# Value blocks of a two-layer macaron kernel: all at full width, in every second slot, ahead of the second score

## What is computed

```python
q = moe_proj(Wq, bq).reshape(B, T, H, D)      # H = 16, D = 8
k = moe_proj(Wk, bk).reshape(B, T, H, D)
v = moe_proj(Wv, bv).reshape(B, T, H, D)
scores = jnp.einsum('bthd,bshd->bhts', q, k) / np.sqrt(D).astype(np.float32)
attn = jax.nn.softmax(scores, axis=-1)
out = jnp.einsum('bhts,bshd->bthd', attn, v).reshape(B, T, C)
return out @ Wo + bo

x = x + 0.5 * _L0_ffn_ref(_layernorm(x), ...)
x = x + _L0_attn_ref(_layernorm(x), ...)
x = x + 0.5 * _L0_ffn_ref(_layernorm(x), ...)
```

## Time and profile before

| what | value |
|---|---|
| median of three runs | 1281.38 us (1278.4 to 1283.0) |
| the profiled execution | 1280.69 us |
| its span, first to last instruction | 1279.0 us, mean granted TensorE clock 0.955 |
| busy over the span | PE 1157.0 us, VectorE 1061.4, ScalarE 941.1, GpSimd 307.7 |
| maximum reductions (L959) | 512, 594.5 us |
| exponentials (L795) | 1024, 545.3 us |
| value matmuls (L1261) | 3584, 317.1 us |
| score matmuls (L1245) | 1024, 309.2 us |
| maximum matmuls (L1230) | 1024, 282.6 us |

### The profile page before, as it was taken

One profiled execution on the slowest core, in us unless ns is written; L12 is line 12 of the kernel. 1 busy time (PEld: TensorE's weight loads), 2 busy tenths in 40 slices (PEclk: granted clock), 3 DMA queues, 4 the chain that ended last, 5 costly groups with the idle time before them and its releaser, 6 DMA issues. The chain is left out here.

```text
span 1279.0 us, 31986 instructions
## 1 busy us (share of the span) xinstructions
PE 1157.0 (90%) x10884; PEld 502.0 (39%) x10884; DVE 1061.4 (83%) x1787; ACT 941.1 (74%) x2001; POOL 307.7 (24%) x535
## 2 busy tenths in 40 slices
PE   4499999998987899999999999998769999999996
PEld 3122222222225555555566565555522222222223
DVE  6899999998987777777755777776589999998997
ACT  3179999998983677777755777775339999998994
POOL 4400000022000354444432444443330000000200
PEclk9689999999997999999999999998869999999998
DMA  4812212354210001000000000000431212244422
GB/s 109 247 32 56 64 52 60 81 88 85 66 41 19 18 23 29 18 17 18 18 18 18 18 18 18 18 18 2 149 99 48 69 47 55 75 79 88 83 48 67
DMA packets 51793, 69.55 MB, mean 54 GB/s; under 512 B 21168, under 2 KB 29296, under 8 KB 51696
## 3 DMA queue, kind: packets, MB, share of 16 engines
q1 hardware_dynamic: 51696, 68.26, 21.7%
HBM read 37.30 MB, written 22.54 MB: 47 GB/s over the span
## 5 line engine op out<-in xcount | busy, mean ns | idle before, releaser
L959 DVE TENSOR_REDUCE neg_max<-ps 128x1 f32<-128x1024 f32 x512 | 594.5, 1213 | 26.6 <-PE ps L1230 22.8
L795 ACT ACTIVATE arena<-ps 128x512 f32<-128x512 f32 x1024 | 545.3, 597 | 84.2 <-PE ps L1245 71.9
L1261 PE MATMUL ps<-arena 128*32 128x256 f32 (+1 forms) x3584 | 317.1, 426 | 25.0 <-ACT arena L795 24.2
L1245 PE MATMUL ps<-arena 50*128 50x512 bf16 x1024 | 309.2, 388 | 6.2 <-DMA arena<-max_dram 5.6
L1230 PE MATMUL ps<-arena 48*128 48x512 bf16 x1024 | 282.6, 397 | 16.8 <-DVE neg_max L959 14.4
L1031 DVE TENSOR_REDUCE a_neg_max<-ps 128x1 f32<-128x129 f32 (+7 forms) x256 | 191.9, 750 | 110.4 <-PE ps L1382 109.4
L634 POOL TENSOR_SCALAR arena<-arena,a_rsum 128x128 f32<-128x128 f32 (+7 forms) x256 | 191.1, 747 | 310.8 <-DVE a_rsum L1050 303.5
L731 ACT ACTIVATE arena<-ps,a_neg_max 128x129 f32<-128x129 f32 (+7 forms) x256 | 189.2, 739 | 51.0 <-DVE a_neg_max L1031 38.5
L1377 PE MATMUL ps<-arena 64*128 64x128 f32 (+6 forms) x512 | 192.6, 457 | 0.0
L1375 PE MATMUL ps<-arena 64*128 64x321 f32 (+7 forms) x512 | 187.9, 450 | 4.9 <-DVE neg_s_null L1062 1.9
L1245 PEld LDWEIGHTS ps<-arena 50*128 50x128 bf16 x1024 | 71.7, 94 | 258.2 <-ACT arena L795 226.3
(11 more groups left out here) (125 smaller groups left out, 820.5 us busy)
## 6 DMA issues: line engine op xcount, KB each, us to landing
arena<-stack_dram SPq DMA_DIRECT2D x128, 192.0 KB, 3.4
stack_dram<-arena SPq DMA_DIRECT2D x48, 256.0 KB, 3.8
o_dram<-arena SPq DMA_DIRECT2D x32, 256.0 KB, 2.1
arena<-arena SPq DMA_DIRECT2D x32, 256.0 KB, 3.6
arena<-o_dram SPq DMA_DIRECT2D x30, 256.0 KB, 4.4
arena<-max_dram SPq DMA_DIRECT2D x256, 1.0 KB
x<-in_L_attn_x SPq DMA_DIRECT2D x2, 512.0 KB, 4.9
max_dram<-max_T SPq DMA_DIRECT2D x64, 8.0 KB, 1.7
```

The source lines that it names most:

```text
L795: nc.scalar.activation(probs[:, t, :], ps[:, EXP_BANK[t], :], ACT.Exp, scale=F_SCALE).then_inc(probs_ready, 1)
L959: nc.vector.tensor_reduce(neg_max[:, g, t:t + 1], ps[:, bank:bank + 2, :].rearrange("p a b -> p (a b)"), AX, ALU.max, negate=True).then_in ...
L1245: ins = nc.tensor.matmul(ps[:, bank, :], stack[rows, g, 1, kt * P:(kt + 1) * P], stack[rows, g, 0, h * HALF:(h + 1) * HALF], start=True, s ...
L1261: ins = nc.tensor.matmul(ps[row:row + 32, PV_BANK, cols], v_unit[:, g, t // 2, :], probs[:, t, cols], start=j == 0 and c0 == 0 and g % 2 == 0,
```

## The change

The value groups 0, 1 and 2 are no longer cut in two. All four groups are full-width blocks of 512 queries: group 3 of the unit before in slot 1, as it was, and groups 0, 1 and 2 in slots 3, 5 and 7, each between that slot's maximum tile and its second score. The even slots have no value block. A group could start in the slot before, once its four exponentials are there; the new table puts it one slot behind that. The evacuation of the output bank moves behind the fourth exponential of a unit, where it stood behind the third. The block behind the last unit is the same one, read from the new table.

```diff
+        VALUES_AT = {kt: ((NT // 2 - 1 if kt == 1 else (kt - 3) // 2, 0, HALF),) if kt % 2 else () for kt in range(NT)}
...
-                    if t == 2 and g == 0 and not first:
+                    if t == 3 and g == 0 and not first:
                         evacuate(1, it - 1)
-                    if t == 2 and g == 2:
+                    if t == 3 and g == 2:
                         evacuate(0, it)
...
                     score_tile(g, it, kt, 0)
                     if ahead:
                         max_tile((g + AHEAD) % NB, it + (g + AHEAD) // NB, kt)
-                    if kt == 1 and not first:
-                        values((g - 1) % NB, it if g else it - 1, NT // 2 - 1, 0, HALF)
+                    for j, c0, c1 in VALUES_AT[kt]:
+                        if kt >= 3:
+                            values(g, it, j, c0, c1)
+                        elif not first:
+                            values((g - 1) % NB, it if g else it - 1, j, c0, c1)
                     score_tile(g, it, kt, 1)
-                    if kt >= 2:
-                        values(g, it, kt // 2 - 1, kt % 2 * (HALF // 2), (kt % 2 + 1) * (HALF // 2))
...
-                values(NB - 1, last, NT // 2 - 1, 0, HALF)
+                for kt in range(2):
+                    for j, c0, c1 in VALUES_AT[kt]:
+                        values(NB - 1, last, j, c0, c1)
```

## The result

The changed kernel takes 1334.78 us (median of four runs, 1329.48 to 1337.94) against 1281.6 for the kernel before (four executions too, one more than in the table above): a ratio of 1.041, 95% interval 1.039 to 1.044. It is slower by 53 us. The prediction said 1329, within 1312 to 1346. The profiled execution is the shortest of the four, 1329.48 us, 48.8 over the 1280.69 of before.

What follows compares the result with a forecast made beforehand. VectorE bounds the kernel before; the change makes a closed 2.60 us chain the bound. 21.5 + 21.9 + 1.3 + 2 x 1.15 + 2 x 0.6 = 48.2 us on 1280.69 gives 1329 us, range 1312 to 1346.

Steps and rivals of the forecast that it cites:

- The chain: Second score, exponential, released bank, next odd slot's value block, second score: 2.60 us for two slots, 10.40 a unit; chance 0.80.
- VectorE's 2.31: VectorE's floor for two slots: a unit's eight maxima and transpose cannot go below 9.23 us, a quarter being 2.31.
- Rival A: Faster: TensorE does 0.7 us a unit less and units fall from 9.55 to 9.23, giving 1265 us; chance 0.09.
- Across units: Over a unit's end the ring closes too, through bank 1, with the same link lengths, so 2.60 us there.
- The late units: Units held by row maxima arriving late from memory: between 0 and +2.5 us in all, +1.3 taken.
- The first units: Each layer's first unit, run at half clock: between nothing and 1.5 us more, +0.6 taken for each layer.
- The last two units of a layer: Units without maxima at a layer's end: said to run at most as much longer, with no term in the sum.
- The 1.15 for a layer's end: VectorE's closing work waits for the last output, whose evacuation leaves at 2.60 instead of 1.45: +1.15 us each layer.
- The evacuation: Output bank's evacuation behind the fourth exponential: TensorE free at 4.15, block due at 4.20, so hidden; otherwise under 2 us.
- B: No change: the ring of scores and blocks holds but comes out near 2.39 for two slots, 1281 us; chance 0.05.
- C: TensorE's brief waits make its clock fall and rise; ten units of sixty at half clock make 1391 us; chance 0.06.
- D: The change doesn't do what it says: none found; sign would be slot 3's block waiting over 0.1 us for the evacuation.

Runs made afterwards that it cites:

- the fastest version: Changed kernel with half-width value blocks, each one slot late between maximum tile and second score, plus output read-backs spread one to a unit: 1257.88 us, ratio 0.981.
- the second run: Changed kernel with its four full blocks moved behind the second score of the odd slots: 1333.97 us, ratio 1.039 to the kernel before.
- the first experiment: Changed kernel with half-width blocks between maximum tile and second score, one slot late, evacuation behind the fifth exponential: 1273.35 us, ratio 0.993 to the kernel before.
- ninth run: Kernel before with only the output read-back transfers spread one to a unit, value blocks untouched: 1275.32 us, ratio 0.995.

## Why the prediction was right, point by point

**The chain.** All four links came out as read from slot 1 of the kernel before: 0.43, 0.65, 0.53 and 1.00, 2.61 and not 2.60. That it closes, and is longer than VectorE's 2.31, is shown from four sides: by width (512, 384, 256), by one link less (the maximum tile), by one link more (the blocks a slot earlier), and by the place, which alone is worth 9 us at most. No run gives the ring a fourth bank, which would be the most direct test. Rival A's gain for TensorE shows in the value matmuls, 42 us less, but no one waited for it. Beside that, the rule that a change of tiling mode drains TensorE, in the Trainium skill's "TensorEngine Tiling (Array Packing)", Key Properties, cannot be the decisive one here: the fastest version has eight blocks a unit and so twice the changes of the slow one.

**Across units** the prediction said that the links are the same. In the loop they are not: 2.69, as the second of two scores that are released together leaves 0.08 behind the first. That is 0.08 for each unit in the loop. Together with the 0.01 in each chain, units came out at 10.5 and not 10.40. From the fourth exponential of unit 1 to that of unit 29, and at the ends of both layers and the start of the second, ScalarE's rows are:

```profile
83.37 2.06 ACT L796 ACTIVATE arena<-ps 128x512 f32<-128x512 f32 x4 [0.45 <-PE ps L1246]
...
377.41 2.07 ACT L796 ACTIVATE arena<-ps 128x512 f32<-128x512 f32 x4 [0.45 <-PE ps L1246]
...
404.58 0.60 ACT L796 ACTIVATE arena<-ps 128x512 f32<-128x512 f32 x1 [0.33 <-PE ps L1246]
...
975.00 2.62 ACT L796 ACTIVATE arena<-ps 128x512 f32<-128x512 f32 x5 [9.87 <-PE ps L1246]
...
1309.75 0.60 ACT L796 ACTIVATE arena<-ps 128x512 f32<-128x512 f32 x1 [0.33 <-PE ps L1246]
```

294.04 us in 28 units are 10.50 each. The same ends in the kernel before:

```profile
372.09 5.35 ACT L795 ACTIVATE arena<-ps 128x512 f32<-128x512 f32 x10 [0.16 <-PE ps L1245]
...
951.55 2.62 ACT L795 ACTIVATE arena<-ps 128x512 f32<-128x512 f32 x5 [9.98 <-PE ps L1245]
...
1255.61 5.35 ACT L795 ACTIVATE arena<-ps 128x512 f32<-128x512 f32 x10 [0.16 <-PE ps L1245]
```

**The sum.** The 29 units of a layer gained 24.3 and 24.8 us, where the prediction had 21.5 and 21.9: this term was sized too small, by the 0.1 above. The late units were given 1.3, between 0 and 2.5, and took nothing: the longer unit hides them whole (the one wait for row maxima left in the trace is ahead of the second layer's first unit, and all units in the loop take 10.4 to 10.5). The first units took 1.8 more and 0.4 less, in place of 0.6 each; this goes with when the clock comes up (8.4 and 8.0 us behind the layer's first exponential before, 11.9 and 5.2 now). The last two units of a layer took 1.5 more.

The 1.15 for a layer's end has a size near this, but not its reason. The evacuation that VectorE's closing work needs did leave later, 0.95 behind its old place in the unit (at 2.40 behind the first exponential; before, 1.45), yet the closing work came 0.7 us earlier in the unit: 10.7 behind unit 30's first exponential (1290.89 to 1301.60) and not 11.4; in the first layer likewise. In both kernels the store of that output stands in SyncE's queue behind four transfers of row maxima, and starts when they have been issued, not when the evacuation is over (at 1245.10 before, at 1293.88 now). These transfers come 0.6 us earlier in the unit than before:

```profile
1245.66 2.56 SPq L378 DMA_DIRECT2D arena<-max_dram  x4
1248.27 0.44 SPq L385 DMA_DIRECT2D o_dram<-arena  x1
...
1292.90 2.56 SPq L379 DMA_DIRECT2D arena<-max_dram  x4
1295.51 0.44 SPq L386 DMA_DIRECT2D o_dram<-arena  x1
...
1301.60 0.69 DVE L980 TENSOR_TENSOR arena<-arena 112x512 f32<-112x512 f32 x1 [3.70 <-DMA arena<-o_dram]
```

So that this term came out near is luck: what made the layer's end longer is the chain in the last two units, which the prediction named beside it and gave no term. The chain that ended last goes through VectorE's closing work in the kernel before, and through these units' last blocks in the changed one.

In all the two layers' scores take 27.7 us longer in the first (310.4 from 67.08 to 377.44, now 338.0 from 67.14 to 405.18) and 25.9 in the second: 53.6, against 48.2 predicted, and the difference of the medians is 53.

**What the sum did not hold.** The profiled execution is only 48.8 longer, since between the layers, where the code is the same, it took 569.8 (405.18 to 975.00) and the one of before 574.1 (377.44 to 951.55), and the part behind the second layer's last exponential 0.6 less. Over the eleven profiles of this study that stretch takes 569 to 574 us, with the stretches at half clock in other places each time. So an execution of this kernel carries some us that no edit made, and the nearness of 48.2 and 48.8 is partly luck: one term too small, one of the right size for another reason, one stretch short.

**The evacuation** is hidden as said, "by a hair": the block of slot 3 in a unit with evacuation follows its first score by the usual 0.53 (220.53 to 221.06), and the old place would have cost 0.2 to 0.28 in every second unit.

**The rivals.** A and B asked for a chain of 2.31 or 2.39; it was 2.61. Two experiments whose chain was brought to 2.4 came within 8 and 13 us of B's time, their late units included, so its threshold was about right. C did not come about in the changed kernel's mid-layer (clock 1.00 in the window above), but it did at the end of a layer in two other runs with full blocks. The clock of the kernel before was not quite without a fall in mid-layer either: it stood at 0.50 from 1174.6 to 1178.0, right behind a wait of 1.39 us for row maxima. D found nothing.

## What to carry to other kernels

Where engines hand tiles round a ring of few buffers, sum the closed chain before the engines' work: from a tile's issue over its consumer and the released buffer back to the next issue in the producer's order. An instruction put into that order ahead of the tile counts with its whole length in the chain, even if it saves its engine work; the answer is to make it smaller or to put it where its inputs are long ready, and to look for a place in today's trace where the new order already occurs once. And when units get shorter, look again at the transfers that used to fit beside them.

## What the runs showed of the hardware that was not expected

- Inside TensorE's loop the second of two matmuls that are released together comes 0.08 us later than in code written out (218.45 less 217.84 against 221.35 less 220.81); the chain adds this up, some 4 us in this kernel.
- With full blocks the granted clock can fall to 0.50 while TensorE is only pausing, at the end of a layer without maximum tiles: in the second run TensorE had idled 0.52, 0.56 and 0.75 us ahead of the first scores at 1283.61, 1286.09 and 1288.75, the clock fell at 1288.7, and it stayed low for 27 us. In the changed kernel's profile the same stretch, with waits of 0.44 to 0.69 in every 2.4 (1298 to 1309), kept its clock.
- Two 256 KB read-backs in one unit can delay a write of 8 KB that is queued later by enough to hold up TensorE. In the kernel before such a write landed 3.4 to 5.3 us after its issue, and TensorE waited up to 1.5 us (up to 1.8 in the first experiment); with one read-back to a unit (ninth run) it landed after 1.4 to 2.4, and TensorE waited for it nowhere past the first unit. In the changed kernel the reads are still doubled, but the write is issued some 5 us behind the second of them (before, in three cases of six, some 3), and landed after 2.9 to 3.4.
